# ScalarE copies batch 0's x and scales the low-rank operand; bias sums run later in batch 1

## The reference

```python
x = x + L0(x)  # two of 8 experts (softmax, top 2) and a shared expert:
               # (gelu(x @ gate) * (x @ up)) @ down, 256 -> 1024 -> 256, weighted by the two shares
x = x + L1(x)  # one expert (argmax): (silu(x @ W_up.T + b_up) * (x @ W_gate.T + b_gate)) @ W_down.T + b_down, width 512
x = x + L2(x)  # x @ (sum_g y[b,g] * weight[g] * mask).T + bias
x = x + L3(x)  # x @ W_base.T + b_base + 2 * sum_e w[b,e] * (x @ As[e].T) @ Bs[e].T, rank 16
```

## Time and profile before

| | |
|---|---|
| median of three runs | 485.47 us |
| profiled execution, own time | 486.02 us |
| its span, first to last instruction | 484.3 us |
| TensorE matmul (PE) busy | 477.4 us, 99% |
| VectorE (DVE) busy | 398.9 us, 82% |
| ScalarE (ACT) busy | 272.5 us, 56% |
| GpSimd (POOL) busy | 33.7 us, 7% |
| granted TensorE clock | full in every slice |
| moved by DMA | 47.33 MB |

### The profile page before, as it was taken

One profiled execution on the slowest core, in us unless ns is written; L12 is line 12 of the kernel. 1 busy time (PEld: TensorE's weight loads), 2 busy tenths in 40 slices (PEclk: granted clock), 3 DMA queues, 4 the chain that ended last, 5 costly groups with the idle time before them and its releaser, 6 DMA issues.

```text
span 484.3 us, 6829 instructions
## 1 busy us (share of the span) xinstructions
PE 477.4 (99%) x2166; PEld 393.3 (81%) x2166; DVE 398.9 (82%) x701; ACT 272.5 (56%) x448; POOL 33.7 (7%) x56
## 2 busy tenths in 40 slices
PE   8999999999999999999999999999999999999997
PEld 7877778888886888888888888888888888888886
DVE  7789888887888889789988979888887799965455
ACT  5547476667526374456556556676765365554432
POOL 0913200000001000200000020000000100000000
PEclk9999999999999999999999999999999999999999
DMA  5988973404245149422491044404049323000002
GB/s 159 199 246 226 205 100 101 131 0 132 66 73 146 45 101 190 144 68 73 125 152 42 1 118 124 127 4 130 1 108 192 94 65 119 13 2 0 0 1 87
DMA packets 112907, 47.33 MB, mean 98 GB/s; under 512 B 66456, under 2 KB 111640, under 8 KB 112872
## 3 DMA queue, kind: packets, MB, share of 16 engines
q1 hardware_dynamic: 109728, 41.30, 34.8%
q0 software_dynamic: 2560, 5.21, 4.4%
q10 hardware_dynamic: 584, 0.39, 0.3%
HBM read 44.79 MB, written 2.10 MB: 97 GB/s over the span
## 4 chain that ended last, share of the span: by engine, by line
PE 82%; DVE 7%; SPq 4%; DMA 3%; issue 2%; ACT 1%; ACTq 0%; DVEq 0%
PE bank_b L1685 6%; PE bank_b L1683 6%; PE bank_b L1684 6%; PE bank_a L1683 6%; PE bank_a L1684 6%; PE bank_a L1685 6%; PE tail L1707 3%; PE tail L1711 3%; PE tail L1708 3%; PE out L1711 3%; PE out L1707 3%; PE out L1708 3%; PE bank_a L1950 3%; PE bank_a L1951 3%; PE bank_a L1952 3%; DMA raw<-in_L_cond_skill_down 2%
## 5 line engine op out<-in xcount | busy, mean ns | idle before, releaser
L712 ACT ACTIVATE hid_hi<-hid 128x512 fp32r<-128x512 f32 x84 | 53.0, 631 | 87.0 <-DVE hid L1008 53.3
L1016 DVE TENSOR_TENSOR hid_lo<-hid,hid_hi 128x512 fp32r<-128x512 f32 x84 | 57.7, 687 | 17.7 <-ACT hid_hi L712 17.6
L1008 DVE SCALAR_TENSOR_TENSOR hid<-bank_b,mine,hid 128x512 f32<-128x512 f32 x64 | 47.4, 741 | 15.9 <-PE bank_b L1685 14.8
L704 ACT ACTIVATE hid<-bank_a 128x512 f32<-128x512 f32 x68 | 40.2, 592 | 34.2 <-PE bank_a L1685 33.3
L997 DVE TENSOR_TENSOR res_lo<-raw,res_hi 128x768 fp32r<-128x768 f32 x36 | 34.2, 950 | 5.1 <-ACT res_hi L691 5.1
L691 ACT ACTIVATE res_hi<-raw 128x768 fp32r<-128x768 f32 x36 | 30.2, 840 | 6.7 <-DMA raw<-in_L_cond_skill_down 6.6
L997 DVE TENSOR_TENSOR w_lo<-raw,w_hi 128x768 fp32r<-128x768 f32 x30 | 28.5, 951 | 2.4 <-ACT w_hi L691 2.3
L1684 PE MATMUL bank_a<-x_lo,res_hi 128*128 128x512 f32 x74 | 28.9, 390 | 0.0
L1683 PE MATMUL bank_a<-x_hi,res_hi 128*128 128x512 f32 x74 | 28.9, 390 | 0.0
L1683 PE MATMUL bank_b<-x_hi,res_hi 128*128 128x512 f32 x74 | 28.8, 390 | 0.0
L1685 PE MATMUL bank_b<-x_hi,res_lo 128*128 128x512 f32 x74 | 28.8, 389 | 0.0
(11 more groups left out here) (357 smaller groups left out, 1322.4 us busy)
## 6 DMA issues: line engine op xcount, KB each, us to landing
raw<-in_L_cond_skill_down SPq DMA_DIRECT2D x64, 128.0 KB, 3.3
raw<-in_L_cond_skill_gate SPq DMA_DIRECT2D x31, 256.0 KB, 3.1
raw<-in_L_cond_skill_up SPq DMA_DIRECT2D x31, 256.0 KB, 3.4
raw<-in_L_cond_shared_down SPq DMA_DIRECT2D x18, 128.0 KB, 3.7
raw<-in_L_cond_shared_gate SPq DMA_DIRECT2D x8, 256.0 KB, 3.5
raw<-in_L_cond_shared_up SPq DMA_DIRECT2D x8, 256.0 KB, 3.8
raw_gate<-in_L_cond_W_gate SPq DMA_DIRECT2D x16, 128.0 KB, 3.2
early<-in_L_cond_weight POOLq DMA_DIRECT2D x2, 1024.0 KB, 9.5
```

Of the source, the lines that this page charges most:

```text
L704: nc.scalar.activation(hid[:, tile_of(g)], bank_a[tile_of(g)][:, :], func, **kw).then_inc(act_ready, 1)
L712: nc.scalar.activation(hid_hi[:, tile_of(g)], hid[:, tile_of(g)], ACT.Copy).then_inc(hid_hi_ready, 1)
L1008: ins = nc.vector.scalar_tensor_tensor(tile, bank, weight, tile, ALU.mult, ALU.mult)
L1016: nc.vector.tensor_tensor(hid_lo[:, tile], hid[:, tile], hid_hi[:, tile].bitcast(F32), ALU.subtract).then_inc(hid_lo_ready, 1)
```

## The change

The addition that makes batch 0's full x goes; instead ScalarE copies the turned x from its PSUM tile, ahead of the split of chunk 2 (`x0_copied`). The scaled low-rank operand is no longer made on VectorE: ScalarE writes its high part with the condition value as the activation's scale, and VectorE its low part in one operation per batch that scales and subtracts. So `b3_y` in `raw_up1` is gone, and SP's load of W_up moves: it follows W_gate, behind the first joint piece, and waits for the two transposes alone. The transposes stand one chunk earlier. In batch 1, step 4 of the L2 mix moves from chunk 3 beside the L1 chunks and the rest shifts by one; step 0 of the next mix goes from chunk 6 to 7; the base sums move from chunk 1 to the last L1 chunk, the weight sums from chunk 1 to 6, the bias columns from chunk 3 to 7. At the third L1 chunk, x of batch 2 and a2 change places on ScalarE and VectorE. Step counts of `t_step` are renumbered.

```diff
...
 X1_TURN_AT, X1_HI_AT, X1_LO_AT = 3, 4, 4
-L3_TURN_AT = 5
+L3_TURN_AT = 4
 L3_OPERAND_AT = 6
...
 BIAS_LOADS_AT = 11
-T_AT = {2: 0, 5: 1, 7: 2, 9: 3}
-T_HI_AT = {6: ((0, 2), (2, 3), (1, 4)), 8: ((3, 5),)}
+T_AT = {5: 1, 7: 2, 9: 3}
+T_HI_AT = {6: ((0, 1), (2, 2), (1, 3)), 8: ((3, 4),)}
 MAIN_AT = 9
...
 CA_LO_AT = {8: 0, 17: 1}
-A_FIRST = {1: (0, 1, 2), 3: (3, 4)}
-A_BESIDE_FIRST = {0: (5, 6, 7), 1: (8, 9)}
+A_FIRST = {1: (0, 1, 2), 3: (3,)}
+A_BESIDE_FIRST = {0: (4, 5, 6), 1: (7, 8), 2: (9,)}
 A_SECOND_SPLIT = 13
-A_SECOND = {6: (0,), 7: (1, 2), 8: (3, 4), 9: (5, 6), 10: (7,), 11: (8,), 12: (9,)}
+A_SECOND = {7: (0, 1, 2), 8: (3, 4), 9: (5, 6), 10: (7,), 11: (8,), 12: (9,)}
 OUT_PLACE = {1: 9, 2: 7}
...
 XSUM_SECOND = 12
-BIAS_BASE_AT = 1
-BIAS_LORA_AT = 1
-BIAS_AT = 3
+BIAS_LORA_AT = 6
+BIAS_AT = 7
 TURN_REST_LO_AT = {0: 2, 3: 3}
...
             def first_l1(n):
-                sp.wait_ge(*((l3_turn, 2), (l3_lo, 1), (l3_lo, 2))[n])
+                sp.wait_ge(*((l3_turn, 2), (l3_lo, 1))[n % 2])
                 load_l1(sp.value_load(chosen[0:1, 2:3], min_val=0, max_val=E - 1), *l1_weights[n])
...
             def later_l1(b):
...
                     first_l1(0)
+                    first_l1(2)
                 if (kind, b, c) == ("joint", 0, 4):
                     first_l1(1)
-                    first_l1(2)
                 if (kind, b, c) == ("own", 1, 6):
...
                 act.wait_ge(l3_f, 1)
-                nc.scalar.activation(b3_y_hi[:, :], b3_y, ACT.Copy).then_inc(l3_hi, 1)
+                for b in range(B):
+                    nc.scalar.activation(b3_y_hi[:, b * D:(b + 1) * D], b3_t[:, :], ACT.Copy, scale=y_lora[:, b:b + 1]).then_inc(l3_hi, 1)
 
             def later_x_hi(b):
...
                         hidden_hi(0, i)
+                        for k in range(KD):
+                            nc.scalar.activation(out_pair[:, k], tail[:, k, :], ACT.Copy).then_inc(x0_copied, 1)
                     if i + SPLIT_AHEAD <= UNIT_AT[0]:
...
                 elif c == 2:
+                    later_x_lo(2)
                     weights_split_lo(0, 2, a2_hi, a2_lo, a2[:, :])
-                    later_x_lo(2)
                 elif c == 3:
                     x_turn_blocks(3)
+                    bias_base()
 
             def stage_bias1(b):
...
             def l3_parts():
...
                 dve.wait_ge(y_in, 16 * E)
-                chain(nc.vector.tensor_scalar(y_lora[:, :], y_rows[:, :], LORA_SCALE, None, ALU.mult))
+                nc.vector.tensor_scalar(y_lora[:, :], y_rows[:, :], LORA_SCALE, None, ALU.mult).then_inc(l3_f, 1)
                 dve.wait_ge(l3_turn, 2)
...
                                                op0=ALU.mult, op1=ALU.add, accum_out=u3[:, :]).then_inc(u3_done, 1)
-
-            def l3_operand():
-
-                for b in range(B):
-                    ins = nc.vector.tensor_scalar(b3_y[:, b * D:(b + 1) * D], b3_t[:, :], y_lora[:, b:b + 1], None, ALU.mult)
-                ins.then_inc(l3_f, 1)
 
             def bias_base():
...
             def l3_operand_lo():
...
                 nc.vector.tensor_tensor(a3_lo[:, :], a3, a3_hi[:, :].bitcast(F32), ALU.subtract).then_inc(l3_lo, 1)
-                dve.wait_ge(l3_hi, 2)
-                nc.vector.tensor_tensor(b3_y_lo[:, :], b3_y, b3_y_hi[:, :].bitcast(F32), ALU.subtract).then_inc(l3_lo, 1)
+                dve.wait_ge(l3_f, 1)
+                for b in range(B):
+                    cols = slice(b * D, (b + 1) * D)
+                    dve.wait_ge(l3_hi, b + 2)
+                    nc.vector.scalar_tensor_tensor(b3_y_lo[:, cols], b3_t[:, :], y_lora[:, b:b + 1], b3_y_hi[:, cols].bitcast(F32),
+                                                   ALU.mult, ALU.subtract).then_inc(l3_lo, 1)
 
...
                         l3_parts()
-                        l3_operand()
                     if i == L3_LO_AT:
...
             def first_combined(part):
 
-                if part == 0:
-                    nc.vector.tensor_tensor(out_pair, x_lo[:, :, 0:S].bitcast(F32), x_hi[:, :, 0:S].bitcast(F32), ALU.add)\
-                        .then_inc(t_step, 1)
-                elif part == 1:
+                if part == 1:
                     dve.wait_ge(x_lo_ready, 1)
+                    dve.wait_ge(x0_copied, KD)
+                    nc.vector.tensor_tensor(out_pair[:, 0], out_pair[:, 0], xs[:, 0], ALU.subtract).then_inc(t_step, 1)
                     dve.wait_ge(t_step, 1)
-                    nc.vector.tensor_tensor(out_pair[:, 0], out_pair[:, 0], xs[:, 0], ALU.subtract).then_inc(t_step, 1)
-                    dve.wait_ge(t_step, 2)
                     nc.vector.tensor_tensor(xs[:, 0], xs[:, 1], xs[:, 0], ALU.subtract).then_inc(t_step, 1)
...
                 elif part == 2:
-                    dve.wait_ge(t_step, 4)
+                    dve.wait_ge(t_step, 3)
                     nc.vector.scalar_tensor_tensor(out_pair[:, 1], sums_flat, -1.0, out_pair[:, 1], ALU.mult, ALU.subtract)\
...
                         later_x_lo(3)
-                    if i == BIAS_BASE_AT:
-                        bias_base()
                     if i == BIAS_LORA_AT:
...
                     pe.wait_ge(tail_free, len(PREPS))
-                    pe.wait_ge(l3_lo, 2)
+                    pe.wait_ge(l3_lo, 1 + B)
                 elif b < JOINT:
```

More of the change, by code:

```diff
@@ L239, in build @@
         b3_t = sb("b3_t", [P, D])
-        b3_y = raw_up1[:, :, :].rearrange("p k h -> p (k h)")
         b3_y_hi = sb("b3_y_hi", [P, B * D], F32R)
@@ L368, in build @@
         x0_turned = sem("x0_turned")
+        x0_copied = sem("x0_copied")
         first_hi = sem("first_hi")
@@ L738, in l1_chunks @@
                     if b == 1 and c == 2:
+                        later_x_hi(2)
                         weights_split_hi(a2_hi, a2[:, :], (a2_step, A_STEPS))
-                        later_x_hi(2)
                     if b == JOINT:
@@ L744, in combined_hi @@
             def combined_hi(b, which):
-                steps = 5 * (b // JOINT)
+                steps = 4 * (b // JOINT)
                 for n, step in which:
@@ L1453, in beside_l1 @@
                 elif c == 1:
-                    dve.wait_ge(t_step, 8)
+                    dve.wait_ge(t_step, 7)
                     nc.vector.tensor_tensor(out_pair[:, 0], out_pair[:, 0], c3[:, :], ALU.subtract).then_inc(t_step, 1)
@@ L1458, in beside_l1 @@
                 elif c == 2:
-                    dve.wait_ge(t_step, 10)
+                    dve.wait_ge(t_step, 9)
                     nc.vector.scalar_tensor_tensor(sums_flat, out_pair[:, 0], -1.0, sums_flat, ALU.mult, ALU.subtract)\
                         .then_inc(t_step, 1)
-                    dve.wait_ge(t_step, 11)
+                    dve.wait_ge(t_step, 10)
                     nc.vector.scalar_tensor_tensor(out_pair[:, 1], sums_flat, -1.0, out_pair[:, 1], ALU.mult, ALU.subtract)\
```

## The result

The changed kernel takes **501.77 us** (median of 4 runs, 500.07 to 502.16) where the kernel before takes 485.71 us beside it: a ratio of 1.033, 95% interval 1.031 to 1.035. The sign of the forecast was right, but its +4.1 us are +16 us, outside the range of 484.4 to 495.

The account below looks back on a forecast made before the run. TensorE, busy 99% of the 484.3 us span, was taken as the bound, so only its standing time counts. The terms 3.9 - 1.96 + 2.2 gave +4.1, 489.6 us; the 8 in 10 range was 484.4 to 495.

Parts of the forecast that it names:

- The transfer that moves: Head of batch 0: W_up queued ahead of the raw piece of chunks 12 and 13 delays its landing, +3.9 us.
- rival B: Head: the delayed piece is caught in a DMA engine held by the u row's store, 5.7 us more, 495.3 us; chance 0.12.
- VectorE's relief in the head: Head: VectorE is some 1.4 us earlier, but TensorE only meets the piece's landing earlier, 0 us.
- ScalarE's copies: Chunk 2 of batch 0: two copies of x hold TensorE some 0.6 us, repaid at later waits, 0 us.
- Batch 1, stalls: Batch 1's L1 chunks: work taken off VectorE removes all of TensorE's stalls there, -1.96 us.
- Batch 1, late bias rows: Output of batch 1: VectorE waits for the late bias rows and TensorE ahead of c_product(1), +2.2 us, bounds 0 and 4.

Follow-up runs that it names:

- experiment 1: Changed kernel with W_up's load alone put back behind the raw pieces of chunks 12 and 13: 490.18 us, ratio 1.0095.
- experiment 8: Changed kernel, W_up still ahead, with all GpSimd loads for the bias sums and the small store held until the split of chunk 14: 493.31 us, ratio 1.017.
- experiment 2: Changed kernel with batch 1's bias sums alone put back to their early chunks, W_up still ahead: 497.02 us, ratio 1.023.
- experiment 10: Changed kernel with W_up's load behind the pieces and batch 1's weight sums and bias columns one chunk earlier (5, 6): 484.74 us, ratio 1.0005.
- experiment 3: Changed kernel with both put back, W_up's load behind the pieces and batch 1's bias sums early: 483.18 us, ratio 0.9962.
- experiment 13: Kernel before the change with only ScalarE's copies of batch 0's x and the combination steps that go with them: 484.51 us, ratio 0.9998.
- experiment 12: Changed kernel with W_up's load and batch 1's bias sums both put back, run once more: 483.28 us, ratio 0.9981.
- experiment 11: Changed kernel with W_up's load behind the pieces and batch 1's weight sums and bias columns two chunks earlier (4, 5): 483.13 us, ratio 0.9978.
- experiment 14: Changed kernel with the three L1 loads that SyncE issues in batch 1 as whole rows: 496.72 us, ratio 1.025.
- experiment 4: Changed kernel with two of the four DMAs of W_up's load ahead of the raw pieces and two behind: 496.0 us, ratio 1.027.

## Why the forecast was wrong, step by step

**The transfer that moves (+3.9 us): right direction, and about right for its own queue.** W_up ahead of the piece costs 4.5 us of landing (experiments 1 and 8) where I took 4.2. What failed is the step from there to "the piece lands at about 58.2": I treated the delay as a shift in one queue and left out what lies at the later place in the other one. GpSimd's loads start at 48 us, and behind them comes the u row's store; with W_up behind, the piece had landed soon after they got going. Delayed into them it lost another 6.9 us. My rival B had this as a straggler at 0.12, with 5.7 us and the small store as its whole cause; the store is 2.35 to 4.2 of the 6.9. B's head of 9.6 us is near the +9.73 measured by luck, from other parts: 11.4 less the 2.65 by which experiment 1 was ahead, and the half clock against the stalls of before. Its 495.3 falls short at the output. Two smaller readings were off as well: W_gate was issued 2.35 us earlier (34.84 against 37.19), not 0.3, though in experiments 2 and 10 it was at 37.42 and 36.81; and in 140 to 146, my row for 158 GB/s, a raw piece is issued too, from 144.85 on.

The Trainium skill's page "DMA: Bandwidth & Descriptors", section "Queues, rings and completion order", which I weighed for the move, says that each DMA engine consumes the descriptors of a ring in order. By that the piece waits for W_up, and the 4.5 us of experiment 8 against experiment 1 agree. The same page's section "Issuing engines are not separate DMA queues" says that transfers of different issuers run on the same 16 DMA engines and interleave. That was the rule to weigh: the runs agree, and here its price is the 6.9 us between experiment 8 and the changed kernel.

**VectorE's relief in the head (0 us): the 1.4 us came, and what reaches the end is small.** Between 37 and 44 us TensorE gains 1.4 us on its twins of before, in the changed kernel and in experiments 1 and 3 alike, and 0.8 in experiment 13 with the copies alone. I wrote that it then only meets the landing earlier. With W_up behind it went further in the traces: the piece landed at 51.7 and 50.6, and experiment 3 is 3.3 us ahead at the end. But the medians of that kernel are only 0.4% and 0.2% below the kernel before (2.2 and 0.9 us, experiments 3 and 12, the second with an interval that touches none). So the term should have been some -1 to -2 us.

**ScalarE's copies (0 us): right.** TensorE has a gap of 0.60 us at chunk 2 (14.22 against 13.74 is 0.48 later); it is still 0.2 us behind at 37 us and 0.4 us ahead at 38. Alone, the copies change no time (experiment 13).

**Batch 1, stalls (-1.96 us): right,** 18.28 us became 16.32.

**Batch 1, late bias rows (+2.2 us): the wait is where I put it, its size was not.** The way of the rows was taken at 17.3 us and measured 19.3 (21.0 in experiment 1): the 1.0 us that I added for a busier queue should have been 3.0, and my nearest row, the u row's 10.4 us, was a case of one small store, while here the broadcast behind it took 6.4 us instead of 4.7 too. The columns' start was right: 192.33 less the head's 9.73 is 182.6, forecast 182.2. The longer way makes 3.95 us of gap.

**A term that was not in the sum: the clock.** The sum priced gaps by their length. The granted clock fell with both, worth 2.6 and 1.65 us, some 4.2 in all, as much as the whole forecast. The trace before had no gap long enough to show it; its clock is 1.00 in every window of the earlier trace rows.

The terms as measured, in the profiled execution: +8.74 (late piece, net of the relief), +0.99 (half clock less stalls of before), -1.96 (stalls), +4.64 (bias rows' gap and small stalls), +1.65 (half clock) = +14.06.

## What to carry to other kernels

A load that is moved ahead in one queue delays what is behind it into a new place: list what all other queues send there, for the DMA engines are shared, and price the collision and not only the shift. A round trip through DRAM (store, wait, broadcast) should be given the time it takes at its new place, here 19 to 21 us and not the 16.3 of the early place; two chunks of margin made the difference between +1.0% and -0.2% (experiments 1 and 11). And a gap on TensorE can cost more than its length: those of 3.6 us and more did, those of 1.6 to 3.2 did not.

## What the runs showed of the hardware

**The clock behind a gap.** Some gaps of TensorE and the granted clock in the stretch behind them:

| gap, us | where | clock behind it |
|---|---|---|
| 1.56, 1.70 | experiment 10 | 1.00, 1.00 |
| 1.62 | experiment 14 | 1.00 |
| 3.18 | experiment 8, head | 1.00 |
| 3.58 | experiment 4, head | 0.50 |
| 3.95 | changed kernel, output | 0.57 over 4 us |
| 5.65 | experiment 1, output | 0.50 |
| 9.97 | changed kernel, head | 0.50 |

The windows of a gap and of what follows it, for experiments 4 and 1:

```profile
55.30:59.10 3.80, 0.45 (x2) 0.03 (x1) 0.47 (x1) 1.35 (x3) 0.00 (x0) 0.98 1.15 261
59.10:61.00 1.90, 1.83 (x4) 1.49 (x5) 1.90 (x4) 1.02 (x3) 0.00 (x0) 0.50 1.26 74
```

```profile
196.40:202.30 5.90, 0.41 (x2) 0.00 (x0) 1.34 (x3) 0.00 (x0) 0.00 (x0) 0.70 0.52 177
202.30:205.50 3.20, 3.20 (x11) 2.81 (x12) 3.20 (x5) 0.63 (x1) 2.12 (x3) 0.50 0.49 165
```

In both the mean clock of the gap itself is already under 1.00: the fall comes while TensorE still stands. In the changed kernel's gap at the output it is not: the window 208.80 to 213.00 has 1.00, and the starts of the matmuls spread only from 213.55 on, 0.6 us after TensorE had begun again. The table is of single gaps.

**The share of the DMA engines says little of what they move.** In the changed kernel 57 to 63 us has a share of 1.06 at 114 GB/s, where the earlier trace rows has a share of 1.01 at 305 GB/s in 41 to 48: the share counts the time that packets take, whatever they move in it. Of the 145 packets of 1 KB that begin in 57 to 59 us, 8 took 3.3 to 4.5 us each; the median is 0.05 us. The window:

```profile
57.00:63.00 6.00, 0.00 (x0) 0.00 (x0) 0.00 (x0) 0.00 (x0) 0.54 (x1) 0.74 1.06 114
```
